# Sorting the edges of a graph layer: positions as a maximum over the counts, and the node-range one-hots moved from ScalarE to VectorE

## The reference

```python
hid = jnp.maximum(x_cat @ a1 + aab1, 0.0)
e1 = jax.nn.leaky_relu((hid @ a2 + aab2)[:, 0], negative_slope=0.2)
w = jnp.exp(e1 - jnp.max(e1))
pooled = jax.ops.segment_sum(w[:, None] * feats[col], row, num_segments=n)
```

## Time and profile before

| | us |
|---|---|
| median of 3 runs (lowest, highest) | 4785.53 (4779.01, 4790.11) |
| profiled execution, its own time | 4788.67 |
| profiled execution, span | 4786.9 |
| busy in the span: PE, DVE, ACT, POOL | 4257.4, 4332.7, 3831.7, 2743.9 |
| the 24 starts of groups in the sort loop, first to last | 157.7 to 1374.9 |
| TensorE's mean granted clock, share of full speed | 0.973 |

### The profile page before, as it was taken

One profiled execution on the slowest core, in us unless ns is written; L12 is line 12 of the kernel. 1 busy time (PEld: TensorE's weight loads), 2 busy tenths in 40 slices (PEclk: granted clock), 3 DMA queues, 4 the chain that ended last, 5 costly groups with the idle time before them and its releaser, 6 DMA issues.

```text
span 4786.9 us, 131994 instructions
## 1 busy us (share of the span) xinstructions
PE 4257.4 (89%) x24114; PEld 3013.5 (63%) x24115; DVE 4332.7 (91%) x24178; ACT 3831.7 (80%) x12983; POOL 2743.9 (57%) x2886
## 2 busy tenths in 40 slices
PE   1599999999986999999999999999999999999990
PEld 1355555555555777777777777777777777777760
DVE  8789899889896999999999999999999999999988
ACT  1588887888875888888888888888888888888884
POOL 5367777677674555555555555555555555555544
PEclk9999999999998999999999999999999999999995
DMA  2133333333336777777777777777777777777757
GB/s 86 43 81 80 82 86 78 79 88 82 76 81 191 225 225 225 226 224 225 222 225 225 224 224 225 224 225 225 224 225 225 224 225 225 225 224 222 222 163 214
DMA packets 266916, 851.80 MB, mean 178 GB/s; under 512 B 107916, under 2 KB 109584, under 8 KB 266861
## 3 DMA queue, kind: packets, MB, share of 16 engines
q0 software_dynamic: 169920, 673.54, 50.6%
q1 hardware_dynamic: 63543, 160.18, 11.1%
q10 hardware_dynamic: 33398, 17.49, 1.4%
HBM read 739.10 MB, written 111.90 MB: 178 GB/s over the span
## 4 chain that ended last, share of the span: by engine, by line
PE 36%; ACT 26%; issue 3%; DVE 2%; DMA 1%; ACTq 0%; POOL 0%; SPq 0%; DVEq 0%; POOLq 0%
ACT z L1165 18%; PE psum L972 15%; PE psum L976 9%; PE psum L959 8%; ACT onehot L1194 3%; ACT onehot_t L1183 3%; PE psum L985 3%; ACT onehot L1198 2%; DMA p_win<-p_table 1%; PE psum L940 1%; DVE z L1692 1%; DVE z L1685 0%; PE psum L996 0%; ACT onehot L1196 0%; DVE z L1708 0%
## 5 line engine op out<-in xcount | busy, mean ns | idle before, releaser
L755 POOL DMA_INDIRECT z<-qf_table,rec x1664 | 1602.8, 963 | 1468.9 <-PE psum L959 996.7
L1165 ACT ACTIVATE z<-z 128x64 f32<-128x64 f32 x6656 | 1651.5, 336 | 0.0
L972 PE MATMUL psum<-p_win,onehot_t 128*128 x9984 | 1407.8, 275 | 93.1 <-ACT onehot_t L1183 66.5
L972 PEld LDWEIGHTS psum<-p_win,onehot_t 128*128 128x128 bf16 x9984 | 967.0, 97 | 540.0 <-issue 214.2
L959 PE MATMUL psum<-z,onehot 128*128 128x260 f32 x3328 | 1030.3, 391 | 4.7 <-DVE acc L1620 4.0
L976 PE MATMUL psum<-z,ident 128*128 128x258 f32 x3328 | 1002.7, 383 | 0.0
L1571 DVE SCALAR_TENSOR_TENSOR z<-z,a_b 128x129 f32<-128x129 f32 x3328 | 881.6, 289 | 5.9 <-issue 5.0
L1571 DVE SCALAR_TENSOR_TENSOR z<-psum,a_b 128x129 f32<-128x129 f32 x3328 | 828.2, 286 | 0.0
L1561 DVE TENSOR_TENSOR z<-z,psum 128x258 f32<-128x258 f32 x1664 | 699.6, 420 | 105.4 <-PE psum L976 105.0
L1620 DVE TENSOR_TENSOR acc<-acc,psum 125x260 f32 x1664 | 702.0, 422 | 25.3 <-PE psum L959 2.7
L696 POOL DMA_INDIRECT sorted_rows<-z x300 | 491.6, 1639 | 326.7 <-DVE z L1450 231.4
(11 more groups left out here) (220 smaller groups left out, 5584.5 us busy)
## 6 DMA issues: line engine op xcount, KB each, us to landing
p_table<-acc SPq DMA_DIRECT2D x100, 338.6 KB
p_win<-p_table SPq DMA_DIRECT2D x100, 338.6 KB
z<-qf_table,rec POOLq DMA_INDIRECT x1664, 4.5
qf_table<-acc SPq DMA_DIRECT2D x75, 339.5 KB
acc<-in_x_dram SPq DMA_DIRECT2D x25, 448.0 KB
z<-in_x_dram SPq DMA_DIRECT2D x20, 560.0 KB
out_dram<-z ACTq DMA_DIRECT2D x20, 560.0 KB
qf_table<-z SPq DMA_DIRECT2D x25, 339.5 KB
```

The lines of the kernel that those rows point to most:

```text
L755: pool.indirect_dma_start(out=z_t[:, o + j, :], out_offset=None, in_=qf_table, in_offset=bass.IndirectOffsetOnAxis(ap=rec[:, o + j, 3:4].b ...
L972: mm = pe.matmul(to, onehot_t[:, j, :], p_flat[:, bass.ds((w % 2) * (3 * ZW) + (part * ZW + o), n)], start=(part == 0), stop=(part == 2 an ...
L1165: op = act.activation(z_t[:, slot, o:o + DO], z_t[:, slot, o:o + DO], ACT.Copy, scale=z_t[:, slot, o + DO:o + HF])
```

## The change

`windows` moves from ACT to DVE and becomes one comparison a quarter in bf16; for it `edge_win` holds every window number twice, as a bf16 pair. In place of the products with the one-hot, `pick` takes the largest of the 100 values: `before` has 8192 (OWN) on its diagonal, so that the edge's own window is 8192 above its position, and positions in a block stay below 5120. The shift leaves again through `CHUNK_AT`. POOL does one more operation on `before`, and PE's first wait counts it.

```diff
-    CHUNK_AT = KC_MAX // 2
+    OWN = 8192
+    CHUNK_AT = KC_MAX // 2 + OWN // S
...
-        edge_win = carve_z(EC)
+        edge_win = carve_z(EC).bitcast(BF16).rearrange("p (c u) -> p c u", u=2)
...
+            pool.affine_select(out=before[:, :], in_=before[:, :], pattern=[[-1, P]], compare_op=ALU.not_equal,
+                               fill=float(OWN), base=0, channel_multiplier=1).then_inc(s_const, 1)
+            pool.wait_ge(s_const, 20)
...
-            pe.wait_ge(s_const, 20)
+            pe.wait_ge(s_const, 21)
...
-            def windows(g, b, j):
-
-                n = (g * PER + b) * 4 + j
-                since(act, s_pos, n - 7)
-                for c in range(j * CH, (j + 1) * CH):
-                    op = act.activation(win_oh[0:EP, b % 2, c, :], iota_win[0:EP, 0, :], ACT.Abs, scale=-1.0,
-                                        bias=edge_win[0:EP, bass.ds((g * PER + b) * CB + c, 1)])
-                op.then_inc(s_win_dist, 1)
-                act.wait_ge(s_win_dist, n + 1)
-                own = win_oh[0:EP, b % 2, j * CH:(j + 1) * CH, :].rearrange("p c w -> p (c w)")
-                act.activation(own, own, ACT.Relu, scale=-1.0, bias=ones_f[0:EP, 0:1]).then_inc(s_oh, 1)
...
-            dve.scalar_tensor_tensor(out=edge_win[0:EP, :], in0=ua, scalar=float(W), in1=ta, op0=ALU.mult, op1=ALU.add).then_inc(s_edge_step, 1)
+            dve.scalar_tensor_tensor(out=edge_win[0:EP, :, :], in0=ua.unsqueeze(2).to_broadcast([EP, EC, 2]), scalar=float(W),
+                                     in1=ta.unsqueeze(2).to_broadcast([EP, EC, 2]), op0=ALU.mult, op1=ALU.add).then_inc(s_edge_step, 1)
...
-                for c in range(CH):
-                    op = dve.scalar_tensor_tensor(out=picked[0:EP, c, :], in0=psum[0:EP, j % 2, c * W:(c + 1) * W], scalar=1.0,
-                                                  in1=win_oh[0:EP, b % 2, j * CH + c, :], op0=ALU.mult, op1=ALU.mult,
-                                                  accum_out=place_f[0:EP, b % 2, j * CH + c:j * CH + c + 1])
-                op.then_inc(s_pos, 1)
+                dve.tensor_reduce(place_f[0:EP, b % 2, j * CH:(j + 1) * CH], psum[0:EP, j % 2, 0:CH * W].rearrange("p (c w) -> p c w", c=CH),
+                                  AX_X, ALU.max).then_inc(s_pos, 1)
+
+            def windows(g, b, j):
+
+                n = (g * PER + b) * 4 + j
+                since(dve, s_count, n - 7)
+                dve.tensor_tensor(win_oh[0:EP, b % 2, j * CH:(j + 1) * CH, :].rearrange("p c (w u) -> p c w u", u=2),
+                                  edge_win[0:EP, bass.ds((g * PER + b) * CB + j * CH, CH), :].unsqueeze(2).to_broadcast([EP, CH, W // 2, 2]),
+                                  iota_win[0:EP, :, :].rearrange("p c (w u) -> p c w u", u=2), ALU.is_equal).then_inc(s_oh, 1)
...
                     if j == 0 and live_b(g, b, -1):
                         slots(g, b)
+                    if live_b(g, b, 1):
+                        windows(g, b + 1, j)
                     if j == 3 and live_b(g, b, -3):
                         row_ids(g, b)
```

More of the change, by code:

```diff
@@ L200, in gnn_layer @@
         hist_m = base_hl[:, 0:2 * HG * HCOL * LO].rearrange("p (b m c n) -> p b m c n", b=2, m=HG, c=HCOL)
-        picked = carve_z(CH * W).rearrange("p (c w) -> p c w", c=CH)
         place_f = carve_z(2 * CB).rearrange("p (b c) -> p b c", b=2)
@@ L281, in gnn_layer @@
         s_scat = sem("s_scat")
-        s_win_dist = sem("s_win_dist")
         s_win_iota = sem("s_win_iota")
@@ L1118, in group @@
                         base_rows(g, b + 1)
-                    if live_b(g, b, 1):
-                        windows(g, b + 1, j)
                     if j == 2 and live_b(g, b, -3):
@@ L1129, in _ @@
             base_rows(0, 0)
-            for j in range(4):
-                windows(0, 0, j)
             sort_loop(act, group)
@@ L1267, in _ @@
             dve.wait_ge(s_edge_step, 7)
-            dve.tensor_copy(ui, edge_win[0:EP, :]).then_inc(s_edge_step, 1)
+            dve.tensor_copy(ui, edge_win[0:EP, :, 0]).then_inc(s_edge_step, 1)
             dve.wait_ge(s_edge_step, 8)
@@ L1477, in group @@
                             work(g + off, w)
+            for j in range(4):
+                windows(0, 0, j)
             sort_loop(dve, group)
```

## The result

The changed kernel takes 4795.1 us (median of 15 runs) beside 4786.5 us for the one before: a ratio of 1.0020, 95% interval 1.0012 to 1.0028, or 8.6 us slower. The direction was forecast, the size was not: 46 us were expected. The profiled execution has a span of 4795.2 us, 8.3 above.

A forecast was written before the change was run, and what follows sets the result against it. No engine is full; DVE and PE take turns in each group. Contention 2.0, ACT -0.3 and clock 0.6 make +2.3 us over 23 groups, +53; with +0.5 and -7, +46: 4832 us against the median, range 4774 to 4874.

The forecast's parts named there:

- The structure: Each group: some 14.5 us of DVE, then some 36 us of PE; DVE's change in q 12 to 15 counts one for one.
- The sums of durations: DVE in q 12 to 15: reduce 0.49 plus one-hots 0.29 less products 0.73, four times, +0.2 us a group.
- The first group: At the first hidden matmul, no longer held up by ACT's one-hots ahead of take_x: -7 us once, between -3 and -9.
- contention term: DVE in q 12 to 15 against POOL's split_p for SBUF: +2.0 us a group, the 0.2 of own work included.
- The walk by strict turns: Hand walk through q 12 to 15 with DVE and POOL alternating on SBUF: +2.4 us, 0.2 included; bounds +0.2 and +4.1.
- The clock term: PE after its wait in q 1: a longer wait leaves more groups at clock 0.93, +0.6 us a group, between 0 and 1.5.
- The ACT term: PE's part, waits at L889 in q 11: ACT relieved of its one-hots, -0.3 us a group.
- The start of the loop: Ahead of the loop: L1264 writes twice as much and POOL has one more small operation, +0.5 us.
- The ports cost nothing new: Rival: in q 12 to 15 the added operation takes over L1434's waits; -0.1 us a group, some 4777 us; chance 0.20.
- PE keeps its clock: Rival: q 12 to 15 shorter by 0.5 us or more, half the groups at 48.3 us; 4751 us; chance 0.08.
- Slow new operations: Rival: on DVE, windows at 0.49 us or the reduce at L1293's rate, +1.6 us a group; 4869 us; chance 0.15.
- PE waiting for the picks: Sign of the slow-operations rival: PE waits at L824, as DVE has more work in q 0 to 11 than it catches up.

The follow-up runs named there:

- e8: The changed kernel, with the one-hots of q 12 to 15 made by ACT, last in each quarter, the other twelve quarters on DVE; 4733.6 us.
- e9: The changed kernel, with DVE making only the one-hots of q 12 to 15 and ACT the other twelve quarters, last in each; 4799.3 us.
- e11: The changed kernel, with POOL's split_p cut to 8 of 516 columns for windows w = 0 and 1 only, which run in q 12 to 15; 4671.1 us.
- e12: The changed kernel, with split_p cut to 8 of 516 columns for w = 2 and 3 only, from the end of q 15 to about q 4; 4792.2 us.
- e3: The kernel before the change, with POOL's four split_p operations on 8 of 516 columns; 4677.0 us.
- e4: The changed kernel, with POOL's four split_p operations on 8 of 516 columns; 4649.6 us.
- e1: The kernel before with only the position by maximum (reduce and diagonal of 8192), one-hots staying on ACT; 4721.3 us, 0.9863 of before.
- e6: The changed kernel, with the reduce of each quarter done twice on DVE, the first into an unused place; 4838.4 us.
- e5: The changed kernel, with the one-hots of each quarter made twice on DVE, the first into an unused place; 4870.4 us.

## Why the prediction was wrong

**The structure held.** A group is some 14.5 us of DVE and 36 us of PE; e8, e9, e11 and e12 show that only what DVE meets in q 12 to 15 counts, up to a few tenths. The sums of durations held too: +0.2 us a group of DVE's own work, +0.15 measured between e3 and e4. Two terms of the +2.3 us a group did not hold, the contention and the clock; +0.44 was measured. The first group gained 8.1 us where 7 were taken: `hidden` starts at 167.06 instead of 173.37.

```profile
165.14 0.59 ACT L1076 ACTIVATE acc<-psum 128x500 f32<-128x500 f32 x1 [56.30 <-DMA base_rows<-z]
...
167.06 3.54 PE L860 MATMUL psum<-acc 128*128 128x500 f32 x4
```

**The step that failed is the contention term.** The forecast took +1.8 us of further waits for SBUF beside the 0.2. Measured, DVE's part less that of the same kernel with a small split is 14.45 - 11.01 = 3.44 us before and 15.26 - 11.16 = 4.10 after: +0.66. The walk by strict turns had wrong where the turns fall, and in how many quarters. It let POOL's cast come in between the one-hots and L1434 in q 12, which put L1434's end 5.8 us after `p_sum`; in the timeline it is 4.9 (4.8 before): the one-hots of q 12 and 13 found POOL not in the way, L1434 took the wait that it had before, and the cast ended under the reduce. The walk's delays of L1434's ends in q 12, 13 and 14 and of the end of `p_sum` in q 15 were 1.0, 1.4, 2.0 and 2.4 us; the means over groups 3 to 23 are 0.03, 0.1, 0.7 and 0.65. Only the step in q 14 came. One pass by hand through one group, with each doubtful turn given to POOL, was put near the middle of the range of +0.2 to +4.1; the measured +0.81 is near its low end. Nor do shorter picks by themselves lengthen the waits for SBUF, as the prediction argued: e1 shortened them in the same way, and its waits fell by 0.9 us. The lock of the Trainium skill (SBUF — State Buffer, SBUF: two separate sides) is what these rows show: L713 of POOL takes 1.64 us beside L1435 in e1 and 1.10 us where nothing holds it up. It does not say whose turn comes next, so it gives no sum of waits by itself: the prediction's 2.4 "strictly by it" was +0.8 in DVE's part.

**The clock term failed too:** +0.6 us a group taken, none measured. The granted clock in PE's part is 0.955 before and 0.956 after. A longer wait of PE did not leave more groups at a low clock: the changed kernel is at 0.95 in most of them, and the one before swings between 0.92 and 1.00. In DVE's part the clock did fall, from 0.974 to 0.955, but there DVE sets the length.

**The ACT term was somewhat too small:** -0.3 taken. At the same clock PE's part fell from 36.20 to 35.75, so -0.45. Together +0.81 - 0.45 = +0.36, and the two parts' sum went from 50.65 to 51.01 (groups 3 to 23). The -0.89 between e3 and e4 holds where PE hardly waits for DVE.

**The start of the loop:** +0.5 taken, +1.5 measured. DVE's doubled operation moved its first histogram one-hots to 34.6, onto POOL's small copies (0.66 and 0.49 us, 0.30 and 0.29 before), and PE's first matmul waits for POOL's last operation on `before`. The 2.9 us that the second group lost, and the 2.2 us behind the last start, were not followed up.

**The rivals.** *The ports cost nothing new*, at 0.20 and 4777, was the nearer one, 18 us off where the forecast was 37. Its mechanism is seen in q 12 and 13, not in q 14, and it had no place for the other 0.66 us of contention a group, the 2.9 us that the second group lost and the 1.5 ahead of the loop. *PE keeps its clock* did not happen here; it did in e1, from half of this change, where DVE's stretch got shorter, as its condition says: the clock in PE's part rose to 0.981, and 0.96 us a group less in that part are 22 of e1's 65 us (the prediction had 28); most of the rest is DVE's part, 23 x 1.90 = 44. *Slow new operations* was wrong: the reduce runs as L1597 does, not as L1293. One of its signs, PE waiting for the picks, came all the same (7.9 us, 3.5 before), in q 1.

In all, one half of the change gains 65 us and the other, alone, loses 29. Together they lose 9 and do not gain 36: of the 45 us between, some 31 lie in DVE's part (+0.81 us a group where the halves add up to -0.52), where the one-hots take back the lead over POOL that the maximum wins in q 13 (L1434 there: 0.86 us in e1, 1.61 after). Most of the rest lies in PE's part, at the lower clock. The one-hots on DVE cost 74 us once the maximum is there, for a relief of ACT that is worth some 10 us here (23 x 0.45) and 20 at best (23 x 0.89).

## What to carry to other kernels

Take a change of two halves apart before costing it as one: here the maximum alone (4721 us, faster than both kernels) and the work that was moved along with it can be had apart, and their effects did not add. Before moving work to an engine, look for the stretch of the loop in which that engine is the one that others wait for, and for what shares a resource with it there; the four one-hots in q 12 to 15 cost nearly as much as all sixteen (4799 and 4795 us), the other twelve some 12 us (4734, against 4721 for the maximum alone). Where the waits of two engines interleave, a walk through one period is one sample and belongs in the range, not in the middle of the forecast.

## What had not been expected of the hardware

In the stretch of q 12 to 15, beside a busy POOL, an added operation on PSUM cost half of its time (e6: 1.96 us added, 0.98 in DVE's part), since waits for SBUF vanish behind it, while one with two SBUF inputs cost its own time and a little more (e5: 1.14 added, 1.20 up to `p_sum` of q 15, 1.49 in DVE's part). So what an operation on DVE adds to such a stretch depends on where its inputs lie as well as on its length. The whole kernel paid more than that for both, 43 and 75 us, in part because they were added in the other twelve quarters too. And 1.0 us of PSUM work less (e1) shortened the stretch by 1.9 us, with one of POOL's operations fewer ahead of DVE from q 13 on. That such gains come in steps of one POOL operation is a reading of this one case, not tested by itself.
